# Routed experts: seven single tiles exchanged for four mixed tiles of two experts' halves, computed in fp32 as two column tiles

## The reference, cut to what matters

```python
gates = xf @ router_w + router_b                       # 2048 x 8
topv, topi = jax.lax.top_k(gates, 2)
probs = jax.nn.softmax(topv, axis=-1)
comb = jnp.einsum('nke,nk->ne', jax.nn.one_hot(topi, E), probs)
h = gelu(jnp.einsum('nd,edh->enh', xf, w1) + b1[:, None, :])   # D=256, HID=512
y = jnp.einsum('enh,ehd->end', h, w2) + b2[:, None, :]
moe_out = jnp.einsum('ne,end->nd', comb, y)
```

## Time and profile before

| | us |
|---|---|
| median of 3 runs (range) | 378.93 (378.81 to 379.04) |
| the profiled execution | 378.79 |
| its span in the trace | 377.1 |
| PE busy | 368.1 (98%) |
| DVE, ACT, POOL busy | 280.7, 239.9, 219.8 |

### The profile page before, as it was taken

The page is one execution under the profiler, slowest core; times in us unless marked ns, Lnnn a source line. Parts: engine busy times, 40 slices in busy tenths (PEclk is TensorE's granted clock), DMA queues, the critical chain, the costliest instruction groups (busy, mean ns, idle before and its releaser), DMA issues.

```text
span 377.1 us, 8869 instructions
## 1 busy us (share of the span) xinstructions
PE 368.1 (98%) x2805; PEld 349.8 (93%) x2806; DVE 280.7 (74%) x612; ACT 239.9 (64%) x538; POOL 219.8 (58%) x268
## 2 busy tenths in 40 slices
PE   8999999999999999999999999999999998999996
PEld 7987989999999899899999989999999997889995
DVE  5799898888988997799899887555655554554486
ACT  2675456556656635787878857666666665677740
POOL 6558775788788762477782245556565654653200
PEclk9999999999999999999999999999999999999999
DMA  7990000000000066502930112213222324650397
GB/s 219 292 350 20 2 30 15 16 27 30 14 14 28 17 241 248 237 4 35 303 115 3 29 44 86 72 56 95 75 87 81 93 79 127 199 138 29 108 352 253
DMA packets 33855, 40.15 MB, mean 106 GB/s; under 512 B 9690, under 2 KB 26524, under 8 KB 33692
## 3 DMA queue, kind: packets, MB, share of 16 engines
q1 hardware_dynamic: 28976, 29.40, 25.3%
q0 software_dynamic: 4768, 10.28, 8.9%
q10 hardware_dynamic: 76, 0.02, 0.0%
HBM read 27.88 MB, written 11.68 MB: 105 GB/s over the span
## 4 chain that ended last, share of the span: by engine, by line
PE 79%; DMA 6%; DVE 5%; issue 3%; ACT 3%; POOL 3%; DVEq 0%; ACTq 0%; POOLq 0%
PE psum L1385 11%; PE psum L1362 11%; PE psum L1278 10%; PE psum L1322 10%; PE psum L1619 8%; PE psum L1525 7%; PE psum L1499 5%; PE psum L1580 4%; DMA y_rows<-ybuf 4%; PE psum L1238 3%; DMA xsl<-y_rows,table 2%; PE psum L1512 1%; PE psum L1604 1%; PE psum L1136 1%; PE psum L1310 1%
## 5 line engine op out<-in xcount | busy, mean ns | idle before, releaser
L762 POOL DMA_INDIRECT y_tok<-ysl,table x39 | 38.9, 997 | 42.0 <-ACT ysl L1047 37.1
L755 POOL DMA_INDIRECT xsl<-y_rows,table x39 | 39.3, 1008 | 32.1 <-PE psum L1385 11.8
L728 POOL DMA_INDIRECT names<-named,pos x32 | 35.2, 1099 | 12.8 <-issue 8.2
L683 POOL TENSOR_TENSOR Eb<-Eb,rinv 128x512 f32<-128x512 f32 x32 | 33.5, 1065 | 11.6 <-DVE rinv L1833 11.6
L1091 ACT ACTIVATE hr<-psum,b_cur 128x256 f32<-128x256 f32 x48 | 20.1, 471 | 22.1 <-DVE b_cur L2128 12.3
L924 ACT ACTIVATE yTb<-psum 128x256 f32<-128x256 f32 x16 | 6.2, 384 | 42.6 <-PE psum L1342 42.6
L1619 PE MATMUL psum<-xsT_hi,w_cur 128*128 128x256 f32 x192 | 31.0, 284 | 0.0
L663 POOL TENSOR_TENSOR half_sum<-Eb 128x512 f32<-128x512 f32 x16 | 20.7, 1292 | 11.5 <-ACT Eb L879 11.3
L2177 DVE TENSOR_TENSOR hr_lo<-hr,hr_hi 128x512 fp32r<-128x512 f32 x24 | 16.6, 693 | 13.3 <-ACT hr_hi L1104 13.0
L1619 PEld LDWEIGHTS psum<-xsT_hi,w_cur 128*128 128x128 f32 x192 | 26.5, 192 | 0.0
L1047 ACT ACTIVATE ysl<-psum,table 128x256 f32<-128x256 f32 x39 | 17.1, 466 | 12.8 <-PE psum L1499 8.7
(11 more groups left out here) (275 smaller groups left out, 1247.6 us busy)
## 6 DMA issues: line engine op xcount, KB each, us to landing
w_raw<-in_L_ffn_w SPq DMA_DIRECT2D x2, 4096.0 KB, 16.8
y_got<-y_tok SPq DMA_DIRECT2D x8, 512.0 KB, 7.6
sw_raw<-in_L_ffn_sw SPq DMA_DIRECT2D x2, 1024.0 KB, 12.3
y_rows<-ybuf SPq DMA_DIRECT2D x16, 128.0 KB, 1.7
sw_lo_kept<-sw_lo SPq DMA_DIRECT2D x1, 2048.0 KB, 8.7
sw_lo<-sw_lo_kept SPq DMA_DIRECT2D x8, 256.0 KB, 3.5
xs_all<-in_x SPq DMA_DIRECT2D x3, 512.0 KB, 13.8
out<-xs_all SPq DMA_DIRECT2D x3, 512.0 KB, 3.1
```

What stands on the lines that cost most here:

```text
L683: nc.gpsimd.tensor_tensor(Eb[q][:, heads, :], Eb[q][:, heads, :], rinv[:, q, heads].unsqueeze(2).broadcast_to([P, H // 2, CTX]), ALU.mult) ...
L728: nc.gpsimd.indirect_dma_start(names, bass.IndirectOffsetOnAxis(ap=pos[:, k, t:t + 1], axis=0), named[:, k, t, :], None).then_inc(scattere ...
L755: nc.gpsimd.indirect_dma_start(into[:, s % 2, :], None, y_rows, bass.IndirectOffsetOnAxis(ap=table[:, s, 0:1].bitcast(I32), axis=0)).then_ ...
L762: nc.gpsimd.indirect_dma_start(y_tok, bass.IndirectOffsetOnAxis(ap=table[:, s, 1:2].bitcast(I32), axis=0), ysl[:, s % 2, :], None).then_in ...
```

## The change

The 15 single tiles become 8, and 4 mixed tiles are added. A mixed tile holds 64 rows of one expert and 64 of another. An expert whose last 128-row tile would hold at most 64 rows takes a half of a mixed tile for them; if there are more single tiles than 8, they are laid over mixed tiles as two halves of one expert.

- DVE's chain gets more rows: a second count of tiles (`any_e`), a third part in `run_e`, `unused` and `passed`, and the block on `spills`, `spilt` and `change`. There are 3 more operations ahead of `hidden_rest(1, 1)` and 15 more behind `columns_rest(2)`.
- SP also stores the high part of the shared weights (2048 KB) and the late half of `yT` (512 KB) to HBM, loads 8 lists `table_mixed`, and for each mixed tile loads by the experts' numbers 2 x 512 KB of `w1`, 2 x 128 KB of `b1` (one row to 64 partitions) and 2 x 512 KB of `w2`, in fp32, into the places of the stored parts. For the first mixed tile these six loads stand ahead of the list of tile 6. Later it brings the stored parts back.
- POOL gathers the rows of a mixed tile (`gather_mixed`) and scatters its result (`scatter_mixed`, with a wait for the store).
- Mixed tile m is spread over pairs 2m+1 and 2m+2 on PE: `mixed_turn` (2 transposes) and `mixed_first` (4 matmuls of 512 columns) in the first, `mixed_back` (4 transposes) and `mixed_second` (8 of 256 columns) in the second. Each matmul has a stationary operand of 64 columns, and the two halves stand at column tiles 0 and 64. They are plain fp32, without a split.
- ACT gets `mixed_columns` (behind the second half's Gelu), `mixed_gelu` and `mixed_output`, DVE `mixed_hidden`, which adds `b1`.
- Semaphores are merged: the twelve late loads have one (`ld_late`), POOL's constants one (`counters`), and others count twice as far.

The core of the diff:

```diff
-SLOT_TILES = TOK * TOPK // P + E - 1
-SINGLES = SLOT_TILES - 2 * DOUBLES
+SINGLES = E
+MIXED = E // 2
+HALF = P // 2
+SLOT_TILES = SINGLES + 2 * DOUBLES
...
+        w1_mixed = at_words("w1_mixed", [P, 2, KD, HID], AT_SW)
+        w2_mixed = at_words("w2_mixed", [P, 2, HC, D], AT_SW + 2 * KD * HID)
+        h_mixed = at_words("h_mixed", [P, HID], AT_LATE_Y)
+        rows_mixed = at_words("rows_mixed", [P, D], AT_LATE_Y + HID)
+        x_mixed = at_words("x_mixed", [P, KD, P], AT_LATE_Y + HID + D)
...
             sp.dma_start(w2_raw[:, :, :, :], w2.rearrange("e (m p) n -> p e m n", p=P)).then_inc(ld_w2, 16)
+            sp.dma_start(sw_hi_kept[:, :], sw_s[0][:, :].bitcast(F32)).then_inc(late_kept, 16)
+            sp.wait_ge(yt_ready, NT)
+            sp.dma_start(yT_kept[:, :], yT_late).then_inc(late_kept, 16)
...
+            def load_mixed_first(m):
+                if m == 0:
+                    sp.wait_ge(acc_psum, EARLY * TPS)
+                    sp.wait_ge(late_kept, 32)
+                else:
+                    sp.wait_ge(pe_mixed, (m - 1) * 4 + HIDDEN)
...
             for s in range(SLOT_TILES):
+                if s == IN_FLIGHT:
+                    for m in range(MIXED):
+                        load_mixed_names(m)
+                if s == DOUBLE0:
+                    load_mixed_first(0)
+                    load_mixed_second(0)
+                for m in range(1, MIXED):
+                    if s == 4 * m + tile_of(3):
+                        load_mixed_first(m)
+                    if s == 4 * m + tile_of(4):
+                        load_mixed_second(m)
...
             for n in range(2):
                 gather(tile_of(3) + n)
+            gather_mixed(0)
             scatter(DOUBLE0 - 1)
             for d in range(1, DOUBLES):
+                m = (d - 1) // 2
+                if d % 2 and 1 <= m <= MIXED:
+                    scatter_mixed(m - 1)
                 for n in range(2):
                     scatter(tile_of(d - 1) + n)
...
+                if d % 2 == 0 and d // 2 < MIXED:
+                    gather_mixed(d // 2)
...
                 kept(0)
                 gelus(1)
+                if u == 0:
+                    mixed_columns(j)
                 kept(1)
...
+            def mixed_turn(m):
+                pe.wait_ge(rm_loaded, m * 16 + 16)
...
+            def mixed_first(m, s):
+                pe.wait_ge(ht_raw, s + 1)
+                pe.wait_ge(w1m_loaded, m * 32 + 32)
+                pe.wait_ge(act_mixed, m * 3 + ACT_COLUMNS)
+                for k in range(KD):
+                    for a in range(2):
+                        tokens = slice(a * HALF, (a + 1) * HALF)
+                        last = nc.tensor.matmul(bank[HM_BANK][tokens, :], x_mixed[:, k, tokens], w1_mixed[:, a, k, :],
+                                                start=(k == 0), stop=(k == KD - 1), tile_position=(0, a * HALF))
...
+            def mixed_second(m, s):
+                pe.wait_ge(ht_raw, s)
+                pe.wait_ge(w2m_loaded, m * 64 + 64)
+                pe.wait_ge(act_mixed, m * 3 + ACT_GELU)
...
+            def mixed_hidden(m):
+                dve.wait_ge(w2m_loaded, m * 64 + 64)
+                dve.wait_ge(pe_mixed, m * 4 + HIDDEN)
+                nc.vector.tensor_tensor(h_mixed[:, :], bank[HM_BANK][:, :], h_mixed[:, :], ALU.add).then_inc(hm_ready, 1)
```

More of the change, by code:

```diff
@@ new lines, in experts_of, with load_mixed_names @@
+            def experts_of(m):
+                for a in range(2):
+                    sp.load(expert_regs[a], emap[0:1, at(HALF_SLOTS.start + 2 * m + a)])
+                return [sp.snap(r, min_val=0, max_val=E - 1) for r in expert_regs]
+            def load_mixed_names(m):
+                for a in range(2):
+                    sp.load(half_regs[a], name_tile[0:1, at(HALF_SLOTS.start + 2 * m + a)])
+                    row = sp.snap(half_regs[a], min_val=0, max_val=2 * NAME_TILES - 1)
+                    sp.dma_start(table_mixed[halves[a], m, :], name_halves[at(row)].rearrange("a p c -> p (a c)")
+                                 ).then_inc(tm_loaded, 16)
@@ L532, in _, with bring_back @@
+            def bring_back(part, lo, done):
+                kept, home = (sw_lo_kept, sw_s[1]) if lo else (sw_hi_kept, sw_s[0])
+                piece = slice(part * SW_WORDS, (part + 1) * SW_WORDS)
+                sp.dma_start(home[:, piece].bitcast(F32), kept[:, piece]).then_inc(done, 16)
             sp.wait_ge(scattered, 16 * TOPK * NT)
@@ L1624, in double @@
                         last.then_inc(h_psum, 1)
+                if u == 0:
+                    mixed_turn(j)
+                if u == 1:
+                    mixed_back(j)
                 if d == 0:
@@ L2035, in _ @@
                 f, d = 1 - f, 2 * d
-            ends, pairs = run_e[f][:, 0, PADE:], run_e[f][:, 1, PADE:]
+            ends, pairs, odd_halves = (run_e[f][:, n, PADE:] for n in range(3))
             in_pairs = run_e[1 - f][:, 1, :]
```

332 lines of the change are left out of this document (229 added, 103 removed).

## The result

The changed kernel takes **426.87 us** (median of four runs, 426.51 to 427.08), the kernel before 378.99 us on the same chip: a ratio of 1.126, with a 95% interval of 1.1235 to 1.1289. The change costs 47.9 us, where I forecast 37. 416 us was 10.9 us short; the time lies inside the range of 398 to 431, but above the 405 to 422 that I gave to the likeliest case alone.

What follows compares the result with a forecast made beforehand. The prediction took PE, busy 98% of the span, as the bound: 378.8 - 24.4 + 3.3 + 6.7 + 46.3 + 5.0 = 415.7, with the median's 0.14 416 us; 398 to 431 was to hold 8 of 10.

Steps and rivals of the forecast that it cites:

- the likeliest case: Whole kernel: the forecast of 416 us with its band of 405 to 422, chance 0.52.
- seven singles: PE's single tiles: seven fewer at 3.48 us each, 24.4 us off PE.
- routing chain: DVE ahead of the shared projection: 18 more small operations, 4.0 us, delay PE by 3.3 us.
- list of tile 6: SP's queue: this list lands late behind six weight loads, so PE waits 6.7 us at tile 5.
- mixed tiles, at full clock: Pairs with mixed tiles: PE's mixed work and its waits there add 46.3 us.
- slow TensorE behind waits: PE after five waits of 5 to 7 us: half clock costs 0 to 10 us in all, taken as 5.
- the rival of the column tiles: mixed_first and mixed_second: column tiles run one after the other, 54.3 us in place of 46.3, 424 us; chance 0.27.
- The column tiles: mixed_first and mixed_second on PE: 1.9 us each if side by side, as taken, 3.5 if not.
- the narrower slack: Behind the routing chain: 0.7 us at the columns of sub 3, against 1.3 at the accumulators, sets PE's delay.
- the weights of later mixed tiles have two pairs' and one pair's time and are hidden: Loads of 1024 KB and 1280 KB for later mixed tiles, 3.7 and 4.7 us, are covered.
- The rival "faster": POOL's gathers run far enough ahead that rows lie ready for PE; mixed tiles cost 17.2 us, 375 us; chance 0.04.
- the rival over 432: More waits than counted: weights late at mixed_hidden, or POOL's wait for a mixed tile's store ahead of scatters; chance 0.07.

Runs made afterwards that it cites:

- lists_ahead: Changed kernel with six lists in flight instead of four and the first mixed tile's weights loaded behind the list of tile 9: 431.57 us against 435.97.
- early_gather: Changed kernel with the mixed tiles' gathers earlier in POOL's order, the first ahead of the gather of tile 6: 421.46 us against 435.97.
- three_moved: all_moved without its change to DVE's order: 390.28 us, a ratio of 1.031 to the kernel before.
- whole_array: Changed kernel with mixed_first and mixed_second on the whole array instead of two column tiles, output not the block's: 443.95 us against 435.97.
- weights_later: Changed kernel with b1 and w2 of mixed tiles 1 to 3 loaded one pair later: 431.59 us against 435.97.
- prompt_again: early_gather with each mixed tile's scatter ahead of its own pair's two gathers, run on another chip: 401.63 us; kernel before 379.42.
- all_moved: prompt_again's kernel plus lists_ahead, mixed_columns ahead of the second Gelu, and sub 1's adds ahead of the chain's last third: 405.73 us, ratio 1.023 to the kernel before.
- clock_fill: Changed kernel with 30 identity transposes on PE ahead of mixed_turn, where PE waited without work: 442.95 us against 435.97.

## Why the prediction was right, and 11 us short

Term by term, in us, the measured ones from the table of points and the rows above. The singles are carried over from the earlier trace rows, and the mixed tiles are what the 60.4 us of the table's rows for pairs 1 to 10 leave beside the clock's 10.4:

| term | forecast | measured |
|---|---|---|
| seven singles | -24.4 | -24.4 |
| late from the start of the span | 0 | +0.7 |
| routing chain | +3.3 | +2.9 |
| list of tile 6 | +6.7 | +5.6 |
| mixed tiles, at full clock | +46.3 | +50.0 |
| slow TensorE behind waits | +5.0 | +12.0 |
| end of the kernel | 0 | +0.6 |
| sum over the kernel before | +36.9 | +47.4 |

**The range held by luck in part.** With the clock at its upper end my sum ended at 421 us. What carried the range on to 431 was the rival of the column tiles, whose mechanism is not there, and the time fell into that part. The case to which I gave 0.52, 405 to 422, missed it.

**The places were right.** The waits at the shared projection, at tile 5, at `rows_mixed` and at `mixed_first` stand where the orders of SP, POOL and ACT put them, and the experiments moved each by moving its cause: the lists (`lists_ahead`), POOL's gathers (`early_gather`), and all of them together brought 47.9 us over the kernel before down to 10.9 (`three_moved`, on another chip).

**The routing chain** came near, with one step wrong. DVE's adds end 4.8 us later (181.33 against 176.54), 4.1 of it the chain, so the 4.0 was right. But I had let the narrower slack decide, 0.7 at the columns of sub 3. The wait stands at the first product, whose slack is 1.3: 4.1 - 1.3 = 2.8, and 2.9 came.

```profile
180.45 0.88 DVE L2188 SCALAR_TENSOR_TENSOR xs_all<-psum,half_tg,xs_all 128x256 f32<-128x256 f32 x2
```

The columns were in time only because PE had meanwhile lost 1.6 us to its half clock.

**The list of tile 6** cost 5.6 and not 6.7, within its bounds of 2.0 and 8.5. The two parts that I had estimated without a row, 1 us for reading two experts and some 4 us for SP's issues, took 0.8 and 4.6 in the trace. `lists_ahead` shows that the wait came from what stood ahead of the list; 3.1 us of it were the weights' transfer.

**The column tiles** came out at 1.94 and 1.95 us, at the end that I had taken from the row tiles of the earlier trace rows; `whole_array` shows the other end, 3.70 and 3.62. The rival with 424 us was nearer to the time, but its mechanism is not there. The ratio is 1.9 for two tiles. The Trainium skill (TensorE: Matmul & The Clock Gate, Part 3, "Measured speedup vs the span model") gives 2.38 for three; no run here has three.

**The clock** is the larger miss, 7 of 11 us. I had 0 to 10 us and took the middle, since the earlier trace rows showed no fall. Each of the four waits at `rows_mixed` costs 2.2 us behind it (1.8 by the two stretches above, and 0.4 at `mixed_turn`, whose successor starts 0.65 to 0.68 us later where it is 0.22 at full clock), 8.8 in all; the wait at tile 5 adds 1.6 (PE is 10.77 us late at that turn, and 18.32 - 5.97 = 12.35 us ahead of the wait in pair 1); and I count the 1.6 us that are added between the first product of sub 2 and the last of sub 5 to it too, as PE's rows stand 0.21 us apart behind the wait of 2.70 us and 0.12 later. The price per wait that I had worked out, 2 us, was right. The 12.0 us lie above even my upper end of 10, since I had counted five waits, and the sixth, 2.7 us at the shared projection, lost the clock too. What failed was taking 5 between two ends of 0 and 10: the row of the start, half the rate after no work, was the evidence, and the clock row of a kernel that never waits is none against it. The Trainium skill (the same page, "HAM oscillation — how this bites in real kernels") has PE start at half the clock behind each wait for a DMA. By that rule the time was 421; the trace agrees, with 0.50 granted for 4.6 us behind a wait of 6.

**The mixed tiles** were 3.7 us too low at full clock. I had let the later gathers land in 2.8 us, as the first one does (262.84 to 265.63). From the second on they take 4.6:

```profile
262.84 0.95 POOL L868 DMA_INDIRECT rows_mixed<-y_rows,table_mixed  x1 [0.30 <-issue]
...
288.69 0.95 POOL L868 DMA_INDIRECT rows_mixed<-y_rows,table_mixed  x1 [0.30 <-issue]
```

to PE at 293.28. Their 1.8 us, three times, are 5.4. The step that failed is "the weights of later mixed tiles have two pairs' and one pair's time and are hidden". They are hidden for those who use them, but they fly beside the gather that PE waits for; SP issues them just ahead of it:

```profile
284.07 1.51 SPq L602 DMA_DIRECT2D h_mixed<-in_L_ffn_b  x2
285.80 1.00 SPq L605 DMA_DIRECT2D w_mixed<-in_L_ffn_w  x2
```

`weights_later` gave the 1.8 us back. Against it, the waits at `mixed_first` were 1.2 us and not 1.6 (4 x 0.4 = 1.6 us less).

**The rival "faster"** priced the same kernel with rows always ready, at 375 us, and called the gathers' place in the queue its decisive point. `early_gather` and `prompt_again` took that point away and reached 401.6. So its mechanism has a second condition that I had not seen: behind the wait for rows stood one for the buffer that `x_mixed` shares with the mixed output. It holds ACT for 1.2 to 1.5 us in three of the four tiles of `prompt_again`, and PE's waits there are 2.6 to 2.8 us where the first is 1.2. I had this only as half a sentence, among the waits of the rival over 432.

## To carry to other kernels

When a full engine is given work that depends on other queues, what counts is where in those queues the new step stands, not how much work it saves: 24 us of matmul went off PE, some 18 came on with the mixed tiles, and 40 us of waiting with them. Moving a new wait away shows the next one behind it, so look for shared buffers and for transfers in flight beside the one that is waited for. And price each wait on TensorE with the slow stretch behind it: a wait of 6 us cost 8 here.

## What the runs showed of the hardware

- Waits of 1.2 us left TensorE's clock at 2.4 GHz (`mixed_first` in 1.94 us behind them). Of those of 2.5 to 2.9 us at `mixed_first` some cost it and some did not: in `prompt_again` the eight records took 3.48 us behind a wait of 2.56, 1.94 behind 2.78 and 3.68 behind 2.76; in `all_moved` 1.94 behind one of 3.06 and 3.56 behind one of 3.10.
- 3.5 us of transposes at the head of a wait put the fall of the clock off, but 2.7 to 4.5 us without work behind them still lost it (`clock_fill`).
- An indirect gather of 128 rows took 2.8 us alone and 4.6 beside 1280 KB of loads on another queue.
- A list of 1.5 KB took 4.9 us behind 2304 KB in the same queue, 1.6 by itself.
- Two fp32 column tiles of 64 run side by side: 1.94 us against 3.70.
- Chips differ by some 5% for the same kernel (379 and 397 us), and on the slower kind ACT has waits of up to 5.25 us that end with nothing that the profile names, one of them for transposes that stood in PE's rows as done. What delays them is open.
